# Running the fourth contraction of a two-layer triangle kernel unit by unit among the residual steps

## The reference

```
# layer 0
zn  = layernorm(x) * w + b
a   = (zn @ W_ap + b_ap) * sigmoid(zn @ W_ag + b_ag) * mask
b   = (zn @ W_bp + b_bp) * sigmoid(zn @ W_bg + b_bg) * mask
out = einsum('bikc,bkjc->bijc', a, b)         # contraction over k, per channel c
x1  = x + out @ W_z + b_z
# layer 1
y     = layernorm(x1) * w + b
left  = sigmoid(y @ left1)  * (y @ left2)
right = sigmoid(y @ right1) * (y @ right2)
p     = einsum('nsre,nkre->nske', left, right) # contraction over r, per channel e
res   = x1 + (layernorm(p) @ out_w) * sigmoid(y @ gate)
```

## Time and profile before

| | us |
|---|---|
| median of 3 runs | 1022.87 (1022.68 to 1027.06) |
| profiled execution, its own time | 1021.16 |
| its span | 1019.4 |
| PE busy | 825.6 (81%) |
| DVE busy | 764.6 (75%) |
| ACT busy | 635.3 (62%) |
| POOL busy | 586.1 (58%) |

### The profile page before, as it was taken

The page is one execution under the profiler, slowest core; times in us unless marked ns, Lnnn a source line. Parts: engine busy times, 40 slices in busy tenths (PEclk is TensorE's granted clock), DMA queues, the critical chain, the costliest instruction groups (busy, mean ns, idle before and its releaser), DMA issues.

```text
span 1019.4 us, 26387 instructions
## 1 busy us (share of the span) xinstructions
PE 825.6 (81%) x9820; PEld 787.8 (77%) x9820; DVE 764.6 (75%) x1851; ACT 635.3 (62%) x866; POOL 586.1 (58%) x409
## 2 busy tenths in 40 slices
PE   4644454577999899986789999898999899989765
PEld 3544454566999799976679999898989899979754
DVE  7999999875499948992890788707980798069796
ACT  5698888655667537742574577546763676257664
POOL 7699999975266306630780244415661567058787
PEclk9798979779999999999999999999999999999999
DMA  4455589977799528968671569856982698876575
GB/s 136 123 166 156 154 264 321 343 261 267 252 277 318 173 67 281 330 179 328 188 242 52 165 210 290 313 194 185 301 253 91 181 303 263 272 235 228 190 232 189
DMA packets 173237, 228.71 MB, mean 224 GB/s; under 512 B 11064, under 2 KB 109624, under 8 KB 171064
## 3 DMA queue, kind: packets, MB, share of 16 engines
q1 hardware_dynamic: 172248, 226.93, 69.7%
q10 hardware_dynamic: 864, 0.12, 0.1%
HBM read 134.73 MB, written 92.27 MB: 223 GB/s over the span
## 4 chain that ended last, share of the span: by engine, by line
PE 40%; DVE 21%; DMA 16%; issue 12%; POOL 5%; ACT 4%; SPq 1%; DVEq 0%; POOLq 0%; ACTq 0%
PE bank L1091 17%; DVE stats L918 6%; PE bank L1071 6%; PE bank L1072 6%; PE ps_w L1121 5%; DMA xin<-in_x_dram 5%; DMA xin<-x 4%; DVE split L962 4%; DVE xc L955 2%; PE ps_t L1106 2%; POOL rstd L645 2%; DMA xcol<-quad 2%; DMA chunk<-xcol 2%; DVE var L925 2%; POOL xin L666 2%
## 5 line engine op out<-in xcount | busy, mean ns | idle before, releaser
L645 POOL TENSOR_TENSOR rstd<-var,minus_half 128x8 f32<-128x8 f32 x192 | 340.8, 1775 | 373.2 <-DVE var L925 371.5
L1091 PE MATMUL bank<-rhs,lhs 128*128 128x128 f32 x2048 | 244.7, 279 | 15.9 <-DVE lhs L898 8.7
L1091 PEld LDWEIGHTS bank<-rhs,lhs 128*128 128x128 f32 x2048 | 235.9, 194 | 19.4 <-DVE lhs L898 8.8
L703 ACT ACTIVATE sig<-bank 128x512 f32<-128x512 f32 x256 | 151.4, 601 | 69.7 <-PE bank L1072 67.2
L730 ACT ACTIVATE xt<-ps_x 128x1024 bf16<-128x1024 bf16 x128 | 131.0, 1023 | 55.4 <-PE ps_x L1132 38.9
L1132 PE MATMUL ps_x<-ident_b,split 128*128 128x128 bf16 x1024 | 84.7, 230 | 94.9 <-DVE split L962 94.8
L955 DVE TENSOR_TENSOR xc<-xc,rstd 128x504 f32<-128x504 f32 (+1 forms) x192 | 140.8, 733 | 23.0 <-POOL xc L659 19.8
L1132 PEld LDWEIGHTS ps_x<-ident_b,split 128*128 128x128 bf16 x1024 | 66.5, 103 | 107.9 <-DVE split L962 107.0
L1071 PE MATMUL bank<-w_rhs,chunk 128*128 128x128 bf16 x1024 | 138.3, 229 | 6.7 <-DVE rhs L890 3.5
L1072 PE MATMUL bank<-w_rhs,chunk 128*128 128x128 bf16 x1024 | 137.5, 229 | 0.0
L1121 PE MATMUL ps_w<-w_out,opair 128*128 128x128 f32 x896 | 122.6, 280 | 18.3 <-ACT opair L722 14.9
(11 more groups left out here) (104 smaller groups left out, 1431.5 us busy)
## 6 DMA issues: line engine op xcount, KB each, us to landing
chunk<-xt SPq DMA_DIRECT2D x90, 512.0 KB, 4.4
xt<-xt SPq DMA_DIRECT2D x80, 512.0 KB, 5.1
xin<-in_x_dram SPq DMA_DIRECT2D x128, 256.0 KB, 4.7
x<-xin SPq DMA_DIRECT2D x64, 256.0 KB, 5.0
xin<-x SPq DMA_DIRECT2D x64, 256.0 KB, 4.8
out_dram<-xin SPq DMA_DIRECT2D x64, 256.0 KB, 4.6
spill<-lhs SPq DMA_DIRECT2D x8, 1024.0 KB, 5.3
chunk<-xcol SPq DMA_DIRECT2D x16, 512.0 KB, 5.6
```

Of the source, the lines that this page charges most:

```text
L645: g.tensor_tensor(rstd[:, m % 2], var[:, m % 2], minus_half[:, :], ALU.pow).then_inc(rooted, 1)
L703: a.activation(sig[:, s], v[:, 0:C, :], ACT.Sigmoid).then_inc(gated, 1)
L1091: last = mm(bank[:, n], operand["lhs"][:, kh, c, :], operand["rhs"][:, kh, c, :], start=kh == 0, stop=kh == HALVES - 1)
```

## The change

Four edits go together. The fourth contraction (q = 3) is not run in 16 ticks of its own, but one unit in each tick of the third quadrant of x steps, in a phase "x in contraction" with the lags of "x with chunks"; the schedule has 16 ticks fewer. As `quad` still holds the result of contraction 2 then, the result of contraction 3 goes to the first k-half of `lhs`, channel by channel, into the memory of the operands that the group just contracted has freed, with even and odd columns apart. The turns of the fourth quadrant read it there with a step of 64 float32 within a partition, and their mix uses weights with interleaved rows (`w_pairs`, two more small loads and a memset at the start). From then on the roles are swapped: the first k-half of the layer 1 `lhs` lies in `quad`, the results of contractions 4 to 6 lie in the first k-half of `lhs`, that of contraction 7 in `quad`. Each restored piece has a semaphore of its own. In the p phases all stages of the p steps come one tick later against the units and chunks. In contraction 0 the last eight z steps stand at ticks 0, 1, 2, 3, 5, 6, 8, 9 instead of 0, 1, 3, 4, 6, 7, 9, 10.

```diff
-P_LAGS = dict(stats=-1, variance=-1, root=-1, centre=-1, norm=0, turn=0, turn_out=1, mix=1, spread=-2,
-              gate=0, gate_out=2, scale=2, load=2, residual=3, store=4, gate_load=-4, project=0, gates=1, make=1)
+P_LAGS = dict(stats=0, variance=0, root=0, centre=0, norm=1, turn=1, turn_out=2, mix=2, spread=-1,
+              gate=1, gate_out=3, scale=3, load=3, residual=4, store=5, gate_load=-3, project=0, gates=1, make=1)
...
-    "x alone": dict(X_LAGS, load=0, add=1, keep=2, stats=2, variance=2, root=2, centre=3, norm=3,
-                    low=4),
+    "x in contraction": X_LAGS,
...
-    "p in contraction": dict(P_LAGS, gate_out=1, spread=-1, gate_load=-4),
-    "p alone": dict(P_LAGS, gate_out=1, spread=-1, gate_load=-4),
+    "p in contraction": dict(P_LAGS, gate_out=2, spread=0, gate_load=-3),
+    "p alone": dict(P_LAGS, gate_out=2, spread=0, gate_load=-3),
...
-    contraction(0, dict(zip((0, 1, 3, 4, 6, 7, 9, 10), range(Z_LATE, 4 * STEPS))),
+    contraction(0, dict(zip((0, 1, 2, 3, 5, 6, 8, 9), range(Z_LATE, 4 * STEPS))),
...
     for n in range(STEPS):
-        tick("x alone", X_BASE + 2 * STEPS + n)
-    contraction(3)
+        tick("x in contraction", X_BASE + 2 * STEPS + n, unit=(3, n))
...
+        def quadrant(q):
+            if q == 3:
+                return lhs_0.rearrange("p (c b n) -> p c b n", c=C, b=2)
+            if q == 7:
+                return quad_0.rearrange("p (g j c) -> p j g c", g=GROUPS_C, c=CG)
+            return (quad_0 if q < 4 else lhs_0).rearrange("p (j c) -> p j c", c=C)
+
+        def operand_of(layer, op, kh):
+            if layer == 1 and op == "lhs" and kh == 0:
+                return quad_0.rearrange("p (c j) -> p c j", j=P)
+            return operand[op][:, kh]
...
+        w_pairs = sb("w_pairs", [P, P])
...
+        loads_diag += [(w_pairs[h:P:2, h * C:(h + 1) * C], W_z) for h in range(2)]
...
+                if q == 4 and n == 0:
+                    act.wait_ge(turned, after(4 * STEPS - 1))
...
+                src = banks[n % 2][:, :, :].rearrange("p b (c j) -> p (b c) j", j=P)
+                if q == 3:
+                    dst = quadrant(3)[:, n * CG:(n + 1) * CG]
+                    src = src.rearrange("p c (n b) -> p c b n", b=2)
+                else:
+                    dst = quadrant(7)[:, :, n] if q == 7 else quadrant(q)[:, :, n * CG:(n + 1) * CG]
+                    src = src.rearrange("p c j -> p j c")
...
+                if h // 2 == 4 * CHUNKS:
+                    dve.wait_ge(turned, after(3 * STEPS - 1))
...
-                        pe.wait_ge(restored[0 if q < 4 else 1], 16 * (u // 2 + 1))
+                        pe.wait_ge(restored[u // 2], 16 * (1 + q // 4))
...
-                    src = quad[:, c0:c0 + COLS, :].rearrange("p (a b) c -> p a (b c)", b=2)
+                    if o < 3 * STEPS:
+                        src = quadrant(0)[:, c0:c0 + COLS].rearrange("p (a b) c -> p a (b c)", b=2)
+                    else:
+                        src = quadrant(3)[:, :, :, c0 // 2:c0 // 2 + COLS // 2].rearrange("p c b n -> p n (c b)")
...
-                    layer = 0
+                    layer, w = 0, w_out[0] if o < 3 * STEPS else w_pairs
```

More of the change, by code:

```diff
@@ L352, in triangle_layers @@
         spilled = [[sem(f"spilled{n}{kh}") for kh in range(HALVES)] for n in range(2)]
-        restored = [sem(f"restored{n}") for n in range(2)]
+        restored = [sem(f"restored{n}") for n in range(GROUPS_C)]
         stats_done, var_done, rooted = sem("stats_done"), sem("var_done"), sem("rooted")
@@ L574, in restore @@
                 sp.dma_start(operand["lhs" if layer == 0 else "rhs"][:, :, cs, :],
-                             spill_dram[layer][:, :, cs, :]).then_inc(restored[layer], 16)
+                             spill_dram[layer][:, :, cs, :]).then_inc(restored[group], 16)
             for m in range(RING):
@@ L619, in _ @@
             g.memset(ident[:, :], 0.0).then_inc(idents, 1)
-            for n in range(2):
-                last = g.memset(w_out[n][:, :], 0.0)
+            for w in (*w_out, w_pairs):
+                last = g.memset(w[:, :], 0.0)
             last.then_inc(zeroed, 1)
@@ L657, in centre @@
                     pool.wait_ge(low_done, after(m - 2))
-                src, lo = (quad[:, c0:c0 + COLS, :], 0) if kind == "p" else (xin[:, m % RING], 1)
+                src, lo = (quadrant(4)[:, c0:c0 + COLS], 0) if kind == "p" else (xin[:, m % RING], 1)
                 g.tensor_tensor(xc[:, h, :, lo:], src[:, :, lo:],
@@ L778, in fill_quadrant @@
                 act.wait_ge(contracted, after(e))
-                dst = last_quad[:, :, n] if q == 7 else quad[:, :, n * CG:(n + 1) * CG]
-                a.activation(dst, banks[n % 2][:, :, :].rearrange("p b (c j) -> p j (b c)", j=P),
-                             ACT.Copy).then_inc(quad_done, 1)
+                src = banks[n % 2][:, :, :].rearrange("p b (c j) -> p (b c) j", j=P)
[5 more added lines that the diff above has]
+                    src = src.rearrange("p c j -> p j c")
+                a.activation(dst, src, ACT.Copy).then_inc(quad_done, 1)
             for t in range(T_END):
@@ L941, in centre @@
                 if m >= LAST_BASE:
[L942 removed]
+                    v.tensor_tensor(xc[:, h].rearrange("p t (g c) -> p t g c", c=CG), quadrant(7)[:, c0:c0 + COLS],
                                     stats[:, h, :, 1:2].unsqueeze(3).broadcast_to([P, COLS, GROUPS_C, CG]),
@@ L1090, in contract @@
                     for kh in range(HALVES):
-                        last = mm(bank[:, n], operand["lhs"][:, kh, c, :], operand["rhs"][:, kh, c, :],
+                        last = mm(bank[:, n], operand_of(q // 4, "lhs", kh)[:, c, :], operand["rhs"][:, kh, c, :],
                                   start=kh == 0, stop=kh == HALVES - 1)
@@ L1105, in turn @@
                 for n in range(COLS // 2):
-                    last = nc.tensor.transpose(ps_t[:, n, :], src[:, n, :], ident[:, :])
+                    last = nc.tensor.transpose(ps_t[:, n, :], src[:, n], ident[:, :])
                 last.then_inc(turned, 1)
@@ L1117, in mix @@
                 else:
-                    layer = 1
+                    layer, w = 1, w_out[1]
                     pe.wait_ge(scaled, after(m - P_BASE - 1))
                 for n in range(COLS // 2):
-                    last = mm(ps_w[:, 2 * n:2 * n + 2, :], opair_of(m)[:, n, :], w_out[layer][:, :],
+                    last = mm(ps_w[:, 2 * n:2 * n + 2, :], opair_of(m)[:, n, :], w[:, :],
                               start=layer == 1, stop=True,
```

11 lines of the change are left out of this document (5 added, 6 removed).

## The result

The changed kernel takes 993.8 us (median of 4, 991.98 to 997.53), the kernel before 1022.77 beside it (median of 4): ratio 0.9722, 95% interval 0.9671 to 0.9772. The prediction was 993. The profiled execution took 993.22 us with a span of 991.6, where the one before had 1021.16 and 1019.4.

A forecast was written before the change was run, and what follows sets the result against it. PE and DVE fill the chunk phases; in the merged region one stretch is DVE-bound, the next PE-bound. Terms sum to -29.3 us from 1021.16, giving 991.9; with the median 1.7 higher, 993.6, stated as 993, range 985 to 999.

The forecast's parts named there:

- merged ticks with the stepped turns: Contraction 3 merged with x steps, through six leftover ticks: 16.5 us gained, 0.5 lost to the fourth quadrant's stepped weight loads.
- start: Start of the kernel: two more small loads ahead of the loads of steps 4 to 6 cost 1.0 us.
- contraction 0: Contraction 0 with z steps closer together: steps come some 4 us earlier, one more unit follows, net -2.5 us.
- contraction 4 to p: First p turn after contraction 4: the 2.81 us wait goes as products and projections run under the root, -3.4 us.
- contraction 5 to p: First p turn after contraction 5: state reached at 799.3 instead of 802.5, less 0.5 for an owed gate product, -2.7 us.
- contraction 6 to 7: Contraction 6 to 7: last fill and unit 0 come ahead of the gate spread and product, -4.7 us.
- p alone: Phase "p alone": DVE's 2.83 us wait for the last fill goes, partly taken by the longer chain behind, -1.0 us.
- The stepped weight loads: Fourth quadrant's turns: 64 float32 weight loads with a step of 256 bytes cost 0.5 us, bounds 0 and 3.2.
- the first rival: Fourth quadrant's turns: each stepped float32 load takes twice its 110 ns, adding 7 us, time 1000; chance 0.08.
- The second rival: P phases: shifting the pair stages only moves the waits one tick later, 11.8 us shrink to 3, time 1002; chance 0.12.
- Rivals 3, 4 and 5: Six steps' leftovers clog next phase, 1002, chance 0.10; serial mix-add chain, 1038, 0.04; units wait for unrestored pieces, 1010, 0.03.

The follow-up runs named there:

- e4: Changed kernel with the pair stages and the z steps back at their old ticks, so the merged ticks and new places alone: 1007.52 us.
- e12: Kernel before with only the pair stages one tick later, and a semaphore for each restored piece: 1010.97 us.
- e2: Changed kernel with the last eight z steps back at their old ticks in contraction 0: 996.8 us.
- e1: Changed kernel with the pair stages of the p steps back at their old ticks: 1002.46 us.
- e7: Changed kernel with the first four loads of x of the merged ticks issued seven ticks earlier, among the restored pieces: 987.33 us.
- e10: e9 with the 16 turns of the fourth quadrant reading adjacent columns (other values than the reference's): 991.24 us.
- e9: Changed kernel with loads of x one tick earlier in the every-other-tick phase and its four rhs spills moved into contraction 4: 991.4 us.
- e3: Changed kernel with the 16 turns of the fourth quadrant reading 128 adjacent columns, not columns 256 bytes apart (other values than the reference's): 993.78 us.
- e8: Changed kernel with contraction 7's first gate chunk loaded five ticks earlier and spread four ticks earlier: 990.97 us.
- e5: e3 with the loads of x in the every-other-tick phase one tick earlier: 988.49 us.
- e6: Changed kernel with only the loads of x in the every-other-tick phase one tick earlier: 993.59 us.

## Why the prediction was right

The total was right within 1 us, and that is partly luck: the prediction's terms sum to -29.3 us, and those that the runs measure to -26.4. Term by term, from the traces (mean of the pairs that differ in one part alone, where there are several):

| term | predicted | measured |
|---|---|---|
| merged ticks with the stepped turns | -16.5 + 0.5 | -15.4 |
| start | +1.0 | not to be told |
| contraction 0 | -2.5 | -2.3 |
| contraction 4 to p | -3.4 | -4.0 |
| contraction 5 to p | -2.7 | -2.7 |
| contraction 6 to 7 | -4.7 | -2.3 |
| p alone | -1.0 | +0.3 |

The three pairs behind the rows of the p steps spread widely, from -1.8 to -5.2 us in the stretch of the second, so these rows hold to 1 or 2 us each.

The merged region is the mean of before less e4 and e12 less e2, contraction 0 of e2 less the changed kernel and e4 less e1. The measured terms sum to -26.4 us of the 28.0 between the two profiled executions; the rest lies in phases that the change leaves alone and is as large as their spread. For the p terms the measured stretches are put in the prediction's terms: contraction 5 takes 31.08 us in place of 29.75, and contraction 6 the same 1.33 more, for work that the shift leaves over, and contraction 7 leaves one step more to "p alone" (the prediction's 1.8 us).

1. *The merged ticks: right, with two errors that cancel.* A tick is 3.82 us (3.81 predicted, of which the sum of the parts was 3.78 and 0.03 an allowance), the wait before the second mix 4.47 (4.7), the leftover ticks 21.98 us (24), the wait for the fill in them 1.12 (1). The lower clock behind the wait cost more than the 1.1 us that I read from one slow unit: mix and unit ran at the lower level throughout, 5.5 us for what takes 2.9 at the upper one, and the turn behind them lost 0.2, so 2.8 in all. (The sum in the timetable is also off by 0.3: mix, unit, turn and mix after 485.6, with the 1.1, end at 491.2 and not at 491.5.) So the stretch to the first projection is 21 us shorter than the 85.90 of the earlier trace rows and not 22.7, as the timetable had it; the six leftover ticks, 2 us faster than forecast, made up for it. e7 showed that the wait and the slow clock both hang on the load behind the restored pieces: 7.5 us. The units and steps share PE without any loss: the nearest row I had used, "p in contraction", was a good one.

2. *The stepped weight loads: the term that was mis-sized.* The prediction said 0.5 us and loads below 200 ns. They take 246 ns, a turn 0.19 us longer, and e10 against e9 gives 3.0 us, just within the bound of 3.2. The mistake was to compare with the float32 loads of the mix, 191 ns, that fit under a pace of 110 ns: those read adjacent columns and say nothing about a step. The bound, 50 ns for each of 64 loads, came out at the right price per load (0.19 / 4 = 48 ns), but by luck: the 50 ns lie between the times that single bfloat16 loads took, and PE's pace did not follow them. Timeline of PE in the kernel before, ten projections apart, in one piece and then with the step of 32 bytes:

```profile
371.84 0.22 PE L1071 MATMUL bank<-w_rhs,chunk 128*128 128x128 bf16 x1
...
372.40 0.22 PE L1071 MATMUL bank<-w_rhs,chunk 128*128 128x128 bf16 x1
...
585.71 0.23 PE L1071 MATMUL bank<-w_rhs,chunk 128*128 128x128 bf16 x1
...
586.33 0.23 PE L1071 MATMUL bank<-w_rhs,chunk 128*128 128x128 bf16 x1
```

That is 56 and 62 ns for each, a difference of 6 ns where the loads differ by 50. The float32 loads differ by 104 ns (246 against 142), and PE's pace by 48. No row that I read could price a stepped float32 load, so the 3.2 was a guess that hit. That the 0.5 did little harm in the total is luck as well: a load of x, stuck behind a spill, waited at the end of that phase anyway, and faster turns alone (e3) gave 0.5 us of the 3.0. The rule of the Trainium skill, "SBUF — State Buffer", section "Door 1: The DMA port swizzle", that every access pays which crosses into another 16-byte line, points the right way (246 against 142 ns here), but the first rival built on it, 7 us, is refuted; 0.16 us per load in place of 0.11 is not double.

3. *Start.* The local effect is there: statistics of step 4 wait 1.84 us for their load where the earlier trace rows has 1.09, and DVE comes to its memset of `quad` at 29.08 us where the kernel before came to it at 28.46. Contraction 0 nevertheless begins at 226.02 as against 226.14, and from 223.5 to 228.9 in the kernels that have the extra loads. The phase wanders by more than the term; it stays open.

4. *Contraction 4 to p and 5 to p: right in place, and in size as far as the pairs tell it.* The turn waits no more, the sum of both is 6.7 us against 6.1. The second rival, that the hole comes back one tick later, is refuted by e1 and e12: what remains for `make` is 1.7 us in five waits at the first place and 2.0 in five at the second.

5. *Contraction 6 to 7: the step that failed.* I had contraction 6 unchanged, the chunk landed as before and no slow clock behind the product. I put the product at 897.2 and unit 15 at 948.1. Moved by the 25.92 us between the two starts of contraction 6 they are at 899.3 and 951.8, so 3.7 us late. Three things make it up. The gate chunk took 8.66 us to land and not 7.91 (0.8). The unit behind the wait of 2.37 us ran at the lower level of the clock, 3.6 us for 2.0 (1.6): the same slow unit stands in the earlier trace rows, and I left it out here. And contraction 6 is 1.3 us longer, since the shift leaves it a turn and a mix of PE more; I had said that such work runs beside the units on idle engines, and PE isn't one (in contractions 4 to p and 5 to p I had counted 0.5 for it). That last part is in the row of contraction 5 in the table. e8, which moves only the chunk and its spread, gets back 2.8 us.

6. *P alone.* The wait for the last fill went, as predicted, and nothing came of it: DVE waits for the mix behind which it now stands. From the end of contraction 7 on the three pairs lost 1.3 to 3.5 us, of which 1.8 is the owed step. Why this stretch varies from 63.0 to 67.2 us between kernels that are alike in it is open: the waits in it are mostly those of the mix for `opair` on ACT, and no run changed them. So the -1.0 and the +0.3 can't be told apart.

Rivals 3, 4 and 5 did not come: six leftover ticks at 3.7 us, no tick over 3.83 behind the lower clock, no piece waited for.

## What to carry to other kernels

Merge a stretch that PE fills with one that DVE fills, and sum PE's starts per tick: here that gave 3.78 us for a pace of 3.82. Then follow each load that the merged work needs back to its queue, because a load issued behind a MB of other traffic costs its wait and the lower clock after it; moving four small loads by seven ticks was worth 7.5 us, about half of the 15.4 that the merge itself brought. An experiment that removes a cost and gains nothing may only have reached the next wait: e3 alone would have priced the stepped weights at nothing, and only with that wait removed on both sides did they show their 3 us.

## What the runs showed of the hardware

- A float32 weight load of 128 columns at a step of 256 bytes took 246 ns, in one piece 142 ns; PE's pace grew by 48 ns each (turns of 0.63 and 0.44 us). A bfloat16 load took 148 ns at a step of 32 bytes and 98 in one piece, and there PE's pace grew by only 6 ns (62 against 56). The time of one load is not its price.
- After 4.47 us of waiting, PE ran at a granted clock of 0.50 for 5.5 us (2.8 us lost); after 2.37 us of waiting, the unit behind the gate product ran at the lower level too (3.6 us for 2.0). When the wait was removed, the lower clock went with it (e7 and e8: 1.00 in those stretches).
- A load of 256 KB took 5.5 to 8.7 us from issue to landing where a spill of 1 MB stood shortly before it in the queue (chains of waits of the changed kernel, e3, e5 and e6), and 10.7 us behind restored pieces; from 482 to 500 in the changed kernel such loads took 2.7.
